# A decoder layer stack on one core: the attention part's order of batches, joint roots, and offsets computed later

## The reference

```python
x = _layernorm(x + attn(x))     # scores = q k^T over rank 64, the same for all 16 heads; softmax; times v; times Wo
x = _layernorm(x + xattn(x))    # expert by token id: silu(x C^T) * (x C^T), times C, C = ctx_2048[e], 4 experts
x = _layernorm(x + ffn(x))      # router picks 1 of 4 experts; silu(x Wg[e]) * (x Wu[e]), times Wd[e], times its weight
```

## Time and profile before

| | |
|---|---|
| time, median of 3 runs | 197.69 us (196.77 to 198.11) |
| span of the profiled execution, first to last instruction | 194.3 us |
| time of the profiled execution itself | not listed apart from the three runs |
| TensorE with products | 176.0 us, 91% of the span |
| VectorE, ScalarE, GpSimd busy | 132.0, 103.3 and 103.0 us |
| mean granted TensorE clock | 0.980 |

### The profile page before, as it was taken

One profiled execution on the slowest core, in us unless ns is written; L12 is line 12 of the kernel. 1 busy time (PEld: TensorE's weight loads), 2 busy tenths in 40 slices (PEclk: granted clock), 3 DMA queues, 4 the chain that ended last, 5 costly groups with the idle time before them and its releaser, 6 DMA issues.

```text
span 194.3 us, 3905 instructions
## 1 busy us (share of the span) xinstructions
PE 176.0 (91%) x969; PEld 140.0 (72%) x969; DVE 132.0 (68%) x406; ACT 103.3 (53%) x274; POOL 103.0 (53%) x130
## 2 busy tenths in 40 slices
PE   1999997999999898989999999999999999999810
PEld 0677775447888655668888788888888888888610
DVE  3269996895678887536554454444799986888950
ACT  3136776725567935537664946643665422455530
POOL 7006356770126884627772168860588810377683
PEclk9999999999999999999999999999999999999975
DMA  5999999246999223146544105444050000011010
GB/s 157 359 336 418 378 366 319 73 139 168 322 334 405 101 85 94 29 130 173 221 149 150 46 0 165 164 162 167 0 162 3 0 0 3 0 57 56 22 62 24
DMA packets 15317, 29.14 MB, mean 150 GB/s; under 512 B 1726, under 2 KB 11968, under 8 KB 15170
## 3 DMA queue, kind: packets, MB, share of 16 engines
q1 hardware_dynamic: 13568, 25.68, 39.4%
q0 software_dynamic: 1440, 3.22, 4.7%
q10 hardware_dynamic: 290, 0.01, 0.1%
HBM read 20.41 MB, written 9.28 MB: 153 GB/s over the span
## 4 chain that ended last, share of the span: by engine, by line
PE 68%; POOL 11%; issue 7%; DMA 5%; DVE 3%; ACT 3%; POOLq 1%; SPq 1%; DVEq 0%; ACTq 0%
PE bank L484 14%; PE bank L486 13%; PE bank L485 13%; POOL out_tokens L473 5%; PE bank L729 4%; PE bank L563 4%; PE bank L652 3%; PE bank L629 3%; POOL rstd L395 3%; DMA arena<-in_attn_w 3%; PE bank L594 2%; PE bank L572 2%; PE bank L511 2%; DMA x_sorted<-buf,slot 1%; PE bank L498 1%
## 5 line engine op out<-in xcount | busy, mean ns | idle before, releaser
L391 POOL TENSOR_TENSOR w_lo<-stage,w_hi 128x512 fp32r<-128x512 f32 x40 | 51.4, 1305 | 44.0 <-ACT w_hi L803 44.0
L912 ACT ACTIVATE gate<-bank 128x256 f32<-128x256 f32 x44 | 17.0, 387 | 48.5 <-PE bank L486 48.5
L1206 DVE TENSOR_TENSOR hid<-bank,gate 128x256 f32<-128x256 f32 x44 | 18.7, 425 | 30.5 <-ACT gate L912 30.2
L484 PE MATMUL bank<-w_hi,xr 128*128 x88 | 35.9, 408 | 1.4 <-DVE xr L1164 0.8
L486 PE MATMUL bank<-w_hi,xr 128*128 x88 | 34.7, 395 | 0.0
L485 PE MATMUL bank<-w_lo,xr 128*128 x88 | 34.7, 394 | 0.0
L484 PE MATMUL bank<-w_hi,hT 128*128 x88 | 28.5, 324 | 0.7 <-DVE hT L1211 0.7
L803 ACT ACTIVATE w_hi<-stage 128x512 fp32r<-128x512 f32 x48 | 28.6, 630 | 0.3 <-PE bank L486 0.3
L486 PE MATMUL bank<-w_hi,hT 128*128 x88 | 24.9, 282 | 0.0
L485 PE MATMUL bank<-w_lo,hT 128*128 x88 | 24.8, 282 | 0.0
L484 PEld LDWEIGHTS bank<-w_hi,xr 128*128 128x128 f32 x88 | 16.6, 189 | 4.4 <-issue 2.3
(11 more groups left out here) (182 smaller groups left out, 329.7 us busy)
## 6 DMA issues: line engine op xcount, KB each, us to landing
stage<-in_w_ffn SPq DMA_DIRECT2D x16, 768.0 KB, 4.5
rows<-x_sorted SPq DMA_DIRECT2D x22, 132.0 KB, 2.3
x_sorted<-padrow SPq DMA_DIRECT2D x1, 2244.0 KB, 10.2
x_sorted<-padrow SPq DMA_DIRECT2D x1, 2112.0 KB, 16.4
buf<-in_x_tok SPq DMA_DIRECT2D x1, 1024.0 KB, 11.0
w_hi<-in_ctx SPq DMA_DIRECT2D x1, 1024.0 KB, 11.5
w_hi<-in_ctxT SPq DMA_DIRECT2D x1, 1024.0 KB, 14.0
x_sorted<-padrow SPq DMA_DIRECT2D x1, 792.0 KB, 12.7
```

The lines of the kernel that those rows point to most:

```text
L391: g.tensor_tensor(out=lo, in0=src, in1=hi.bitcast(F32), op=ALU.subtract).then_inc(split_lo, 1)
L484: mm(dst, xhi, whi, start=start, stop=False)
L912: a(gate[:, (T + j) % 2, :], fA[j % 2][:, 0:FQ], ACT.Silu).then_inc(silu_done, 1)
L1206: v.tensor_tensor(out=hid[:, (T + j) % 2, :], in0=fA[j % 2][:, FQ:2 * FQ], in1=gate[:, (T + j) % 2, :], op=ALU.mult).then_inc(h_done, 1)
```

## The change

The four steps that compute the offsets of the middle layer's weights leave the front of VectorE's list and stand, as `middle_offsets()`, ahead of batch 3, behind the norms of batch 2 (the third). The two roots of a batch become one instruction over two columns, which waits for both variances; both norms wait for it. On TensorE `turn(2)` and `mix(2)` move ahead of `z_of(3)`, `scores(3)` stands between them, and the first of the four router products stands between `turn(3)` and `mix(3)`. ScalarE's list follows: `copy_qk(3)` now stands ahead of `exps(2)`, `copy_z(3)` ahead of the last copy into `aT`, and the splits are dealt out anew. Three idle products fewer stand on TensorE behind the attention. Of VectorE's eight low parts four stand ahead of `hidden(0)`, two behind it and two behind `hidden(1)`.

```diff
-        ACT_SPLITS = [2, 1, 3, 2, 2, 2]
+        ACT_SPLITS = [2, 1, 3, 1, 2, 2, 1]
...
+            def roots1(b):
+                pool.wait_ge(var_ready, 2 * b + 2)
+                g.tensor_tensor(out=rstd[:, b % 2, :], in0=mv[:, b % 2, :, 1], in1=mhalf[:, 0:2],
+                                op=ALU.pow).then_inc(rstd_ready, 1)
...
             for b in range(BATCH):
-                for i in range(2):
-                    root(LN1 + 2 * b + i, b % 2, i)
+                roots1(b)
                 for i in range(2):
                     scatter1(2 * b + i)
...
+            def router_product(h, k):
+                if k == 0 and h == 0:
+                    pe.wait_ge(d_ctxn, 16)
+                    pe.wait_ge(wrc_ready, 1)
+                    pe.wait_ge(qk_copied, 2 * BATCH)
+                if k == 0 and h == 1:
+                    pe.wait_ge(z_copied, BATCH)
+                last = mm(pMT[h].rearrange("p (e f) -> p e f", e=2), wrc[:, k, :], ctxn[:, 2 * h:2 * h + 2, k, :],
+                          start=k == 0, stop=k == DK - 1)
...
             def ctx_router():
                 pe.wait_ge(route1, 1)
+                router_product(0, 1)
+                router_product(1, 0)
+                router_product(1, 1)
...
-                        idle_products(4)
+                        idle_products(3)
...
-            for b in range(BATCH):
-                turn(b)
-                if b + 2 < BATCH:
-                    qk_of(b + 2)
-                mix(b)
-                if b + 2 < BATCH:
-                    z_of(b + 2)
-                    scores(b + 2)
+            turn(0)
+            qk_of(2)
+            mix(0)
+            z_of(2)
+            scores(2)
+            turn(1)
+            qk_of(3)
+            mix(1)
+            turn(2)
+            scores(3)
+            mix(2)
+            z_of(3)
+            turn(3)
+            router_product(0, 0)
+            mix(3)
             ctx_router()
...
-            idle_products(5)
+            idle_products(3)
...
+            copy_aT(0)
+            exps(1)
+            copy_qk(2)
+            splits(ACT_SPLITS[2])
+            copy_z(2)
+            copy_aT(1)
+            copy_qk(3)
+            exps(2)
+            splits(ACT_SPLITS[3])
+            copy_aT(2)
+            splits(ACT_SPLITS[4])
+            exps(3)
+            splits(ACT_SPLITS[5])
+            copy_z(3)
+            copy_aT(3)
+            splits(ACT_SPLITS[6])
...
             def row_norm(b, i):
-                dve.wait_ge(rstd_ready, LN1 + 2 * b + i + 1)
+                dve.wait_ge(rstd_ready, b + 1)
...
             for b in range(BATCH):
+                if b == BATCH - 1:
+                    middle_offsets()
                 inverse_sums(b)
                 row_moments(b, 0)
                 row_moments(b, 1)
...
+            los = iter(LO_BY_DVE)
+            for _ in range(LOS_BEFORE):
+                low_part(next(los))
             for i in range(T):
                 hidden(i)
+                for _ in range(LOS_BEHIND[i] if i < len(LOS_BEHIND) else 0):
+                    low_part(next(los))
```

More of the change, by code:

```diff
@@ L232, in route_kernel @@
         out_ready = sem("out_ready")
-        LN1, LN3 = 0, CHUNKS
+        LN3 = CHUNKS
         PIECES = CHUNK // PIECE
         LO_BY_DVE = range(4, 12)
+        LOS_BEFORE, LOS_BEHIND = 4, [2, 2]
         def wait_los(eng, end):
@@ L391, in split, with root3 @@
                 g.tensor_tensor(out=lo, in0=src, in1=hi.bitcast(F32), op=ALU.subtract).then_inc(split_lo, 1)
-            def root(n, buf, i):
-                pool.wait_ge(var_ready, n + 1)
-                g.tensor_tensor(out=rstd[:, buf, i:i + 1], in0=mv[:, buf, i, 1:2], in1=mhalf[:, 0:1],
+            def roots1(b):
+                pool.wait_ge(var_ready, 2 * b + 2)
+                g.tensor_tensor(out=rstd[:, b % 2, :], in0=mv[:, b % 2, :, 1], in1=mhalf[:, 0:2],
+                                op=ALU.pow).then_inc(rstd_ready, 1)
+            def root3(t):
+                pool.wait_ge(var_ready, LN3 + t + 1)
+                g.tensor_tensor(out=rstd[:, t % 2, 0:1], in0=mv[:, t % 2, 0, 1:2], in1=mhalf[:, 0:1],
                                 op=ALU.pow).then_inc(rstd_ready, 1)
@@ L467, in _ @@
                             split(k)
-            root(LN3, 0, 0)
+            root3(0)
             for t in range(T):
                 if t + 1 < T:
-                    root(LN3 + t + 1, (t + 1) % 2, 0)
+                    root3(t + 1)
                 pool.wait_ge(out_ready, t + 1)
@@ L533, in ctx_off @@
                 return offs[t]
+            def router_product(h, k):
[7 more added lines that the diff above has]
+                          start=k == 0, stop=k == DK - 1)
+                if k == DK - 1:
+                    last.then_inc(mT_done, 1)
             def ctx_router():
-                pe.wait_ge(d_ctxn, 16)
-                pe.wait_ge(wrc_ready, 1)
                 pe.wait_ge(route1, 1)
[L540 to L544, removed]
+                router_product(0, 1)
+                router_product(1, 0)
+                router_product(1, 1)
                 pe.wait_ge(tables, 1)
@@ L820, in _, with copy_aT @@
             splits(ACT_SPLITS[1])
-            for b in range(BATCH):
+            def copy_aT(b):
                 act.wait_ge(t_done, b + 1)
@@ L1024, in _ @@
             step(v.tensor_reduce(out=slot_of[:], in_=count3[:].rearrange("p s j -> p j s"), axis=AX.X, op=ALU.add))
[L1025 to L1031, removed]
             maxes(1)
@@ L1072, in row_norm, with middle_offsets @@
                                        op0=ALU.subtract, op1=ALU.mult).then_inc(row_ready, 1)
+            def middle_offsets():
+                step(v.tensor_tensor(out=has_slot, in0=slot_of[:].unsqueeze(1).broadcast_to([P, T, BLOCKS]),
+                                     in1=tile_no1[:].unsqueeze(2).broadcast_to([P, T, BLOCKS]), op=ALU.is_equal))
+                step(v.tensor_tensor(out=has_slot, in0=has_slot,
+                                     in1=expert_of[:].unsqueeze(1).broadcast_to([P, T, BLOCKS]), op=ALU.mult))
+                step(v.tensor_reduce(out=expert[:], in_=has_slot, axis=AX.X, op=ALU.add))
+                v.scalar_tensor_tensor(out=off1[:], in0=expert[:], scalar=float(DK * CW), in1=ones_f[:, 0:T],
+                                       op0=ALU.mult, op1=ALU.mult).then_inc(tables, 1)
             dve.wait_ge(d_x, 16)
             for b in range(BATCH):
+                if b == BATCH - 1:
+                    middle_offsets()
                 inverse_sums(b)
@@ L1165, in fxlo, with low_part @@
                                 op=ALU.subtract).then_inc(xlo_done, 1)
-            for k in LO_BY_DVE:
+            def low_part(k):
                 _, _, src, hi, lo = all_pieces[k]
@@ L1244, in finish_norm @@
             def finish_norm(t):
-                dve.wait_ge(rstd_ready, LN3 + t + 1)
+                dve.wait_ge(rstd_ready, BATCH + t + 1)
                 if t >= 2:
```

## The result

The changed kernel takes 200.42 us (median of four runs, 200.37 to 200.73); the kernel before, run beside it, 197.23 (196.10 to 198.11). The ratio is **1.017, 95% interval 1.0135 to 1.0207**: slower by 3.2 us, where 0.8 was forecast and 200.1 was the upper end of the range. In every run here the time is the span plus 1.8 to 2.0 us. The profiled execution of before (span 194.3) thus took 196.1, its fastest, and that of after (span 198.6) took 200.4, close to its median.

The account below looks back on a forecast made before the run. The prediction took the middle layer's tiles reaching TensorE as the bound, with early and late paths level. Late path: 0.4 (sums) + 0.6 (joint root) - 0.2 (scatter) = 0.8; 197.69 + 0.8 = 198.5 us, range 196.6 to 200.1.

Parts of the forecast that it names:

- the late one: Path through batch 3's mix, moments, root, norm, scatter and read back to tx(3): 0.8 us later, at 47.8.
- TensorE's new order: TensorE's attention part: mix(2) 2.5 us earlier at 28.6, mix(3) at 33.65 instead of 34.27.
- The offsets at batch 2: VectorE, behind batch 2's norms: four offset instructions take 1.85 us unstalled, bounds 1.7 and 3.4.
- Rivals 1 and 3: Offsets on VectorE: 1, they fill a wait for mix(3), 196.8 us, chance 0.2; 3, they stall again, 200.1, chance 0.1.
- Taking them out at the front gives nothing back: VectorE's front: removing the offsets gains nothing, since TensorE waits for nobody between 25.12 and 30.
- Batch 1's sums can start with mix(1)'s first result, 25.12 + 1.24 = 26.36: VectorE's queue at batch 1: row sums can begin 1.24 us behind mix(1)'s start.
- the size of the joint roots: GpSimd's root over two columns: 0.15 to reach it plus 0.55 there; norm(6) 0.6 us more late at batch 3.
- Scatter(7) is half free of them and lands 0.2 sooner: GpSimd's last scatter: four low parts of VectorE beside it instead of eight, so it lands 0.2 us sooner.
- The early path: Tiles 0 to 2: tile 0 arrives about 0.9 us earlier, tx(0) at 41.5 to 41.6, up(2) ends at 46.0.
- rival 2: TensorE's clock falls in the new 1.8 us gap before tx(3): +1.5 us on top, 200.0 us, chance 0.15.
- It decides from the point where the first of these passes what the tail shows: Rival 2's condition: gaps of 1.8 us before tx(3) and about 1.1 before tx(0), against the tail's thin stretch.

Follow-up runs that it names:

- e1: Changed kernel with each row's own root again, two a batch over one column; median 197.5 us, ratio 1.003 to the kernel before.
- e7: Kernel before with only the four offset instructions moved behind the third norms; median 199.0 us, ratio 1.010.
- e12: Changed kernel with offsets behind the last norms, roots apart and three more idle products ahead of tile 0; median 196.5 us, ratio 0.997.
- e3: Changed kernel with joint roots and the offsets' move both undone, leaving the reordering; median 196.5 us, ratio 0.998 to the kernel before.
- e8: The reordering alone (roots apart, offsets at the front) plus three more idle products ahead of tile 0; median 196.3 us, ratio 0.998.
- e14: Changed kernel with five more idle products ahead of tile 0 alone; median 200.3 us, ratio 1.018 to the kernel before.
- e2: Changed kernel with the four offset instructions back at the front, ahead of maxes(1), roots still joint; median 198.3 us, ratio 1.006.
- e6: Kernel before with only the joint roots added; median 198.2 us, ratio 1.007.
- e10: The reordering alone with three more idle products ahead of tile 0 and all eight low parts behind the hidden steps; median 196.6 us, ratio 0.996.
- e5: Changed kernel with five more idle products ahead of tile 0 and nine between up(2) and tx(3); median 199.2 us, ratio 1.010.
- e4: Changed kernel with eight idle products between up(2) and tx(3); median 200.2 us, ratio 1.018 to the kernel before.
- e11: Changed kernel with the offsets behind the last norms, their tables awaited at the first tile; median 199.0 us, ratio 0.999.
- e13: Changed kernel with offsets behind the last norms and five more idle products ahead of tile 0; median 197.2 us, ratio 0.999.

## Why the prediction was wrong in size

The side was right, and so was the path: the late one sets `tx(3)`, and the early one waits. From mix(1)'s start, `tx(3)` was forecast 22.7 us away (47.8) against 21.9 before; it came at 24.1.

- **TensorE's new order: right.** mix(2) and mix(3) start 3.72 and 8.76 behind mix(1), by the forecast 3.5 and 8.5; neither is waited for by VectorE.
- **The offsets at batch 2: right.** 1.75 us for 1.85, unstalled, and from batch 2's first sum to batch 3's it is 6.22 where the forecast had 6.2. Rivals 1 and 3 fell with it.
- **"Taking them out at the front gives nothing back": right, but it costs.** With the offsets gone, VectorE comes to the slot step while GpSimd runs its low part and stands there 1.12 us, for 0.17 without it (before at 22.02); in before the stall was in an offset step. Batch 1's sums stand 0.27 later behind mix(1) in e1, e7 and e12, which have that, than in before, e3 and e8. I had let them start with mix(1)'s first result; e14, alone of its kind, does (1.22): its slot step starts 0.01 us ahead of the low part and takes 0.17. It still takes 21.90 from there.
- **The failed step: "Batch 1's sums can start with mix(1)'s first result, 25.12 + 1.24 = 26.36", and with it the size of the joint roots.** I walked VectorE's queue from batch 1 on and put what stands ahead of it at nothing, the root of batch 0 and the moved stall. The sums began 2.00 behind mix(1), 0.76 later than forecast: 0.42 of that is the root of batch 0 (e2, e6 beside before), 0.27 the slot step, and 0.07 was there in before already (1.31 for 1.24). The forecast's walk held waits for a root of 0.1, 0.7 and 0.7 at batches 1 to 3 and none at batch 0; the four are 0.34, 0.46, 0.84 and 0.84, 2.48 for 1.5. At batch 1 the step from sums 1 to sums 2 is 4.67, not the forecast 4.29, since GpSimd was still scattering when the variances were ready. And the root over two columns takes 0.72 to 0.76, not the 0.57 of one: nearer one column's price than the bound of 1.15, but not it (I had read it from a subtraction over 512 columns beside a power over one, two different operations). Joint roots cost 1.1 us of late path on before (e6) and 1.66 on after (e1); the 0.6 charged at batch 3 was never their whole price.
- **"Scatter(7) is half free of them and lands 0.2 sooner": near in size, by luck.** It landed 5.61 behind norm(6)'s start, for 5.75 in before, 0.14 sooner, but because scatter(6) took 1.12 for 1.29. Scatter(7) itself took 1.44 and landed in 2.91, as in before, though the four low parts (41.67 to 44.16) stood beside its first 0.6 us alone. It is short in two profiles: in e10 (0.97), with no low part beside it, and in e12 (0.98), where it starts 0.01 us ahead of the first low part. Scatter(6) starts 0.04 and 0.05 us ahead of it in e1 and e7 and takes 1.05. With e14's slot step these are four cases in which the one that started first wasn't held up; no run was made to test that. The Trainium skill's page "SBUF — State Buffer" (Who interferes with whom) has a VectorE instruction with two SBUF inputs contend with GpSimd instructions that read SBUF, and infers that a `tensor_tensor` doesn't hold up the generation of descriptors. e8's and e10's pairs (2.66 and 2.01 us) show scatters longer beside VectorE's low parts. The scatter at 35.94, beside the offsets, wasn't: it took 1.04, no more than e10's 1.04.
- **The early path: size wrong.** `tx(0)` comes 17.45 behind mix(1), by the forecast 16.4, as the same delays at batches 0 to 2 push its scatters back too. The wait ahead of it was 1.26 for the 1.1 that rival 2 named.
- **Rival 2, chance 0.15, came on top.** "It decides from the point where the first of these passes what the tail shows": with 1.4 us more of late path the second gap was 2.19 and not 1.8. Its price of 1.5 holds: 1.3 by e5. Behind a gap of 1.36 (e1) it didn't come, nor behind e14's 1.80, each in its one profile. With the roots apart two of e1's ten clocks show a fall, with joint roots all four of after's, so the mis-sized late path and the clock weren't independent cases, and my range added neither to the other.

The sum: to the forecast 0.8 come 0.76 ahead of sums 1 (2.00 for 1.24), 0.38 at batch 1, 0.14 at batch 3's root and 0.11 behind it, 1.4 in all (batch 2's longer root and the shorter offsets cancel), and 1.3 of clock: 3.5, against 3.2 measured. What lies around the span was taken as 3.4 and is 1.8, which changes nothing: the 0.8 was in effect added to the median.

What stays open: where the clock falls in the unprofiled executions of e1, e2, e7 and e14; and what posts the semaphore at 66 us late. That delay gives TensorE two waits, of 0.57 to 0.63 and of 0.92 or 0.93 us, 2.3 us apart, in all twelve profiles that have it, and the clock fell behind them in four (e2, e3, e5, e14) and held in eight. e3 and e8 have the same two waits at the same times (65.3 and 67.6), and only e3 lost the clock, so something that these views don't show decides. The four profiles without the delay have one wait there, of 0.58 to 1.03 us, and no fall.

## What to carry to other kernels

Merging two small operations on a helper engine saves it an issue but takes the pipelining away: the first consumer now waits for both inputs and the whole operation. That price falls due at every batch whose queue is on the path, so walk the queue from the first batch, and from the instructions ahead of it. When a change widens a gap of TensorE, price the clock as part of the same case and not as a separate mishap, and try idle products there before judging the change. A stall beside another engine's long operation needn't vanish when its victim moves: here the next instruction in the queue inherited it in eight profiles of nine.

## What the runs showed of the hardware

- The granted clock fell to 0.50 for 3.4 us behind waits of 1.22 (e4), 1.52 (e2), 1.79 (e11) and 2.19 us (after), and not behind 1.26 (after, ahead of tile 0), 1.36 (e1) or 1.80 (e14). So the length of the single wait doesn't decide. With idle products in the gap before tile 0 and no long one before `tx(3)`, all 39 executions of e8, e10, e12 and e13 kept a clock of 0.980 or more.
- A power over 128x2 on GpSimd takes 0.72 to 0.76 us, over 128x1 0.54 to 0.60, but 0.72 as well in before, e1 and e7 beside VectorE's norm.
- An indirect scatter of 128 rows occupies GpSimd 0.97 to 1.08 us where no low part of VectorE is under way when it starts (1.21 for the first of all), 1.11 to 1.47 where one is. Where the last one of its group took 0.97 or 0.98 it landed 2.4 us after its issue (e2, e4, e10 to e13), where it took 1.42 to 1.44, 2.9.
- VectorE steps of 0.17 to 0.53 us stood 1.09 to 1.18 us beside GpSimd's low part (1.27 us).
- The start-up alone moves everything behind it by up to 2 us from execution to execution: absolute times of two profiles say less than distances between anchors in one.
